# Segment maxima of attention logits: one VectorE instruction per chunk in place of scaled copies by ScalarE and a wide maximum

## The reference, cut to what matters

```python
h = x @ Wn.T + bn
e = edge_attr @ We.T + be
a = jax.nn.leaky_relu(jnp.sum((xj + ee) * attn, axis=-1), 0.01)   # xj = h[src]: one logit per edge
m = jax.ops.segment_max(a, dst, num_segments=N)                    # the maximum of each destination
a = jnp.exp(a - m[dst])
```

## Time and profile before

| | us |
|---|---|
| median of three timed runs | 4665.79 |
| the profiled execution, device time | 4637.7 |
| its span, first to last instruction | 4635.9 |
| logits stage, VectorE's first looped expand to its last reduction | 2416.29 to 2899.99 |
| VectorE busy from 2416 to 2900 | 362.95 |
| ScalarE busy in the same stretch | 356.56 |

### The profile page before, as it was taken

One profiled execution on the slowest core, in us unless ns is written; L12 is line 12 of the kernel. 1 busy time (PEld: TensorE's weight loads), 2 busy tenths in 40 slices (PEclk: granted clock), 3 DMA queues, 4 the chain that ended last, 5 costly groups with the idle time before them and its releaser, 6 DMA issues. The chain is left out here.

```text
span 4635.9 us, 88448 instructions
## 1 busy us (share of the span) xinstructions
PE 3555.2 (77%) x19416; PEld 2665.9 (58%) x19417; DVE 2679.8 (58%) x9145; ACT 1686.4 (36%) x5377; POOL 1075.3 (23%) x828
## 2 busy tenths in 40 slices
PE   5555558888887759999973333689999699998978
PEld 4333337777776658878862222578888344444444
DVE  7999989999987751112237777777766400000523
ACT  1555532334444430000027776577775100000110
POOL 1888888888881000000000000000000000000000
PEclk9999999999998879999985555899999899999989
DMA  3444434567776664435535554443332163442064
GB/s 103 110 114 113 110 75 125 154 196 210 207 215 236 239 220 119 133 110 153 135 116 173 160 156 142 133 139 119 119 102 68 37 221 122 169 155 70 1 253 138
DMA packets 435572, 656.94 MB, mean 142 GB/s; under 512 B 97532, under 2 KB 291767, under 8 KB 435362
## 3 DMA queue, kind: packets, MB, share of 16 engines
q1 hardware_dynamic: 354306, 526.63, 36.9%
q10 hardware_dynamic: 53040, 121.95, 7.2%
q0 software_dynamic: 28144, 7.36, 2.4%
HBM read 438.84 MB, written 216.02 MB: 141 GB/s over the span
## 5 line engine op out<-in xcount | busy, mean ns | idle before, releaser
L989 POOL DMA_INDIRECT slots<-all_B,put_index x800 | 1051.9, 1315 | 342.9 <-issue 238.3
L1725 POOL DMA_DIRECT2D out_dram<-all_B x7 | 8.6, 1222 | 2231.6 <-DVE all_B L1709 2231.6
L965 PE MATMUL put_ps<-put_right_in,put_left_in 128*128 128x125 f32 x2380 | 350.5, 298 | 140.9 <-ACT put_left_in L835 140.3
L765 DVE TENSOR_SCALAR put_hot<-all_iota_bf,put_words_in 128x125 bf16<-128x125 bf16 x2400 | 443.3, 310 | 3.3 <-DMA put_words_in<-slots 3.3
L1220 PE MATMUL lm_ps<-lm_v,lm_node 125*128 x1220 | 169.9, 184 | 328.7 <-DVEq L1087 126.9
L1185 ACT ACTIVATE lm_raised<-lm_hot,srt_words 128x125 f32<-128x125 bf16 x1200 | 360.3, 385 | 140.5 <-DVE lm_top L1100 64.6
L965 PEld LDWEIGHTS put_ps<-put_right_in,put_left_in 128*128 128x128 f32 x2380 | 306.6, 204 | 169.7 <-ACT put_left_in L835 159.7
L835 ACT CAST put_left_in<-put_hot 128x640 f32 (+1 forms) x238 | 172.6, 725 | 633.2 <-issue 316.2
L2262 DVE TENSOR_TENSOR upd_pre<-upd_po,upd_bias 125x512 f32<-125x512 f32 x25 | 17.3, 692 | 630.2 <-PE upd_po L2193 630.2
L1835 PE MATMUL att_ps<-att_right,att_left 128*125 128x125 f32 x2380 | 313.1, 285 | 67.0 <-ACT att_right L1856 63.6
L969 PE MATMUL put_ps<-put_right_out,put_left_out 128*128 128x125 f32 x2380 | 345.9, 298 | 0.7 <-DVE put_right_out L773 0.6
(11 more groups left out here) (346 smaller groups left out, 5967.7 us busy)
## 6 DMA issues: line engine op xcount, KB each, us to landing
c_T<-counts SPq DMA_DIRECT2D x255, 312.5 KB, 2.9
pair<-put_T ACTq DMA_DIRECT2D x125, 625.0 KB
hot<-put_hot SPq DMA_DIRECT2D x480, 160.0 KB
att_ring<-hot SPq DMA_DIRECT2D x240, 320.0 KB, 3.2
all_A<-in_edge_attr_dram SPq DMA_DIRECT2D x100, 448.0 KB
lm_planes<-src_rows SPq DMA_DIRECT2D x123, 320.0 KB, 3.7
counts<-put_T ACTq DMA_DIRECT2D x125, 312.5 KB
lm_hot<-hot SPq DMA_DIRECT2D x120, 320.0 KB, 3.0
```

Source lines behind the costliest of these rows:

```text
L765: ins = v.tensor_scalar(hot[:, h, t, c * S:c * S + P], k["iota_bf"][:, :], words_in[:, j, c, t:t + 1], None, ALU.is_equal)
L965: ins = t_.matmul(tile(1, c), left_in[:, c, :], right_in[:, c, :], start=False, stop=False, skip_group_check=True)
L989: nc.gpsimd.indirect_dma_start(slots, bass.IndirectOffsetOnAxis(index[:, C * g + j:C * g + j + 1], 0), stage[:, C * g + j, :], None).then_ ...
```

## The change

VectorE reads the bf16 one-hots itself. `greater(g)` now issues ten instructions: `tensor_scalar` (times logit) in a block's first group, else `scalar_tensor_tensor` (times logit, then maximum with `lm_top`, in place). ScalarE's loop, the tile `raised` and the semaphore `lifted` are gone. SP's turn has another order: it announces the planes of group g+1 right behind the load of planes g+3, then waits for `grouped` (VectorE's own maxima of group g-3), and loads the hot rows of group g+1, where it had loaded those of g+2.

```diff
@@ sync
-                for j in range(2):
-                    load_hot(j, j)
+                load_hot(0, 0)
...
                         load_planes(g + 3, j + 3)
-                        sp.wait_ge(lifted, g + 1)
-                        sp.sem_inc(passed, 1)
-                        if not last or j < 2:
-                            load_hot(g + 2, j + 2)
                         sp.wait_ge(landed[(j + 1) % RING], 16 * (i + (j + 1) // RING) + 16)
                         sp.sem_inc(arrived, 1)
+                        sp.wait_ge(grouped, g)
+                        sp.sem_inc(passed, 1)
+                        if not last or j < 3:
+                            load_hot(g + 1, j + 1)
                         sp.wait_ge(hot_landed[j], 16 * i + 16)
                         sp.sem_inc(hot_arrived, 1)
@@ vector
                 def greater(g, first):
-                    lift = raised[:, ds(g % 2, 1), :].rearrange("p a n -> p (a n)")
-                    dve.wait_ge(lifted, g + 3)
+                    dve.wait_ge(hot_arrived, g + 1)
                     dve.wait_ge(grouped, g + 2)
-                    if first:
-                        ins = v.tensor_copy(top8[:, :], lift)
-                    else:
-                        ins = v.tensor_tensor(top8[:, :], top8[:, :], lift, ALU.max)
+                    for c in range(G):
+                        one = hot[:, ds(g % RING, 1), c * S:c * S + P].rearrange("p a n -> p (a n)")
+                        at, best = logit[:, ds(G * g + c, 1)], top8[:, c * P:(c + 1) * P]
+                        if first:
+                            ins = v.tensor_scalar(best, one, at, None, ALU.mult)
+                        else:
+                            ins = v.scalar_tensor_tensor(best, one, at, best, ALU.mult, ALU.max)
                     ins.then_inc(grouped, 1)
@@ scalar
-                act.sem_inc(lifted, 2)
-                with act.Fori(0, turns_of(act, k)) as i:
-                    for j in range(RING):
-                        g = RING * i + j
-                        act.wait_ge(ready, g + 1)
-                        act.wait_ge(hot_arrived, g + 1)
-                        act.wait_ge(grouped, g + 1)
-                        for c in range(G):
-                            ins = nc.scalar.activation(raised[:, j % 2, c * P:(c + 1) * P], hot[:, j, c * S:c * S + P], ACT.Copy,
-                                                       scale=logit[:, ds(G * g + c, 1)])
-                        ins.then_inc(lifted, 1)
```

More of the change, by code:

```diff
@@ L1003, in phase_logits @@
         node = s.sb("node", [L, 2, G * L], bf16)
-        raised, top8, tops = s.sb("raised", [L, 2, G * P]), s.sb("top8", [L, G * P]), negated
+        top8, tops = s.sb("top8", [L, G * P]), negated
         v3, rest, z = s.sb("v3", [P, NB, 3], bf16), s.sb("rest", [P, NB]), s.sb("z", [L, G])
@@ L1018, in phase_logits @@
         split, chain_sem = s.sem("split"), s.sem("chain")
-        expanded, looked, summed, ready, lifted, grouped = (
-            s.sem(n) for n in ("expanded", "looked", "summed", "ready", "lifted", "grouped"))
+        expanded, looked, summed, ready, grouped = (
+            s.sem(n) for n in ("expanded", "looked", "summed", "ready", "grouped"))
         joined, passed, turned, ended = (s.sem(n) for n in ("joined", "passed", "turned", "ended"))
```

## The result

| | before | after |
|---|---|---|
| timed median, us | 4669.93 | 4853.98 |
| profiled execution, device time, us | 4637.7 | 4856.24 |
| logits stage, first looped expand to last reduction, us | 484 | 657 |
| VectorE busy in the stage, us | 363 | 528 |
| ScalarE busy in the stage, us | 357 | 0 |

The ratio of the times is 1.0395, with a 95% interval of 1.0362 to 1.0428: slower by 4.0%, 184 us. The kernel before was timed once more beside the new one, hence 4669.93 in place of 4665.79. Its run of 5393.38 us was a slow one, which the median holds and the ratio leaves out.

A forecast was written before the change was run, and what follows sets the result against it. Before, VectorE and ScalarE pace the logits stage in a ring through SyncE; after, VectorE alone. Groups 461.5 + first groups 119.5 + block ends 67.2 - 0.3 = 648 us against 484: +164, 4830 us, range 4785 to 4875.

The forecast's parts named there:

- Ten chunks: VectorE's ten narrow instructions per group: starts 0.26 us apart, 2.68 us in all, bounds 1.72 and 3.44.
- The start and the turn: VectorE's step: 0.45 us from last logit instruction's start to first chunk, 0.45 us idle behind the last chunk.
- The first group's: A block's first group, multiply only: 4.78 us, with 2.55 for ten chunks; times 25 is 119.5 us.
- rival 3: bf16 input makes chunks start 0.17 us apart, ten take about 1.9 us: -95 us, 4735; chance 2%.
- Block ends: VectorE's reduction at a block's end stays: 2.47 us, 0.15 ahead, 0.63 behind; 2.80 more, 24 times, 67.2 us.
- The sum: Logits stage built from VectorE's steps: 648 us against 484, +164 us, 4830 on the timed median.
- SyncE's new order: SyncE's changed turn costs nothing: hot rows issued about 15 us ahead, landing in 3.0; planes covered.
- a ring with ScalarE: Logits stage before: VectorE waits 57.5 us for SyncE, SyncE 299 for ScalarE, ScalarE 112 for VectorE.
- Hidden sequencer work (1): VectorE's address work stays hidden: group 4.18 us, stage 573 us, +89, 4755; chance 4%.
- Chunks that don't overlap (2): Each VectorE chunk waits for the one ahead to end, costing 0.344 us: +91 us more, 4921; chance 4%.
- late hot rows (4): Hot-row loads, issued one group nearer their use, exposed 3.0 us in each of 119 groups: +357, 5187; chance 1%.

The follow-up runs named there:

- e3: The changed kernel with all chunks reading one constant tile and fixed logit columns, no register instruction ahead of a chunk: 4724.45 us, one execution.
- E5: The kernel before, with SyncE announcing the planes of group g+1 before it waits for ScalarE's copies: 4580.80 us, ratio 0.9877.
- e4: The changed kernel with SyncE's old sequence, planes of group g+1 announced last in its turn: 4911.32 us, ratio 1.0500.
- e1: The changed kernel with two wide VectorE instructions (multiply, then maximum) in place of ten narrow ones: 4780.73 us, ratio 1.0238.

## Why the prediction held, point by point

**The account of the 174 us.** The change is two edits of opposite sign. SyncE's new sequence by itself takes 484 to 422 us, -62. The ten fused chunks take that to 657, +235. Of these, 551 - 422 = 129 stay when no addresses are computed (the datapath's part: 2.68 us for ten against 1.46 for one wide maximum, 2.03 against 0.81 in a first group), and 106 are the sequencer's register instructions and loop turn. The split holds for these variants; e3 also took the reading of the ring away.

**Ten chunks** were put at 2.68 us from a neighbouring loop. They took 2.76. The starts were the expected 0.26 apart but for one, between the fifth and the sixth chunk, which was 0.34 (in the step at 2593.68 us); ten chunks take 2.76 or 2.77 in 83 steps. In e3 that gap is gone and ten take 2.68, so it comes with the computed addresses or the ring; which of the two is open. The mixed types changed nothing, as argued from the earlier trace rows.

**The start and the turn** were put at 0.45 and 0.45. The start measured 0.46. The turn was 0.51 behind fused chunks and 0.31 behind a first group's, 42.4 / 93 = 0.46 on average, so that the mean came out close is in part luck. There was luck in the source as well: the profile puts the idle time of line 1898 down to a wait for line 1909, and I read it as sequencer work. Here it is "issue", and e3 shows that it is the sequencer's; what it was at line 1898 no run tested.

**The first group's** 4.78 us measured 2591.89 - 2587.22 = 4.67, as the turn behind it had 0.31 us idle and not 0.45. Its 2.55 us for ten chunks came out exactly. The working there names 0.15 us as line 765's distance and rival 3 names 0.17; with that line's median duration of 253 ns it is (1.72 - 0.253)/9 = 0.16. The sum uses neither. **Block ends** came out as before: 2.46 and 0.62 us.

**The sum** had the stage at 648 us, measured 657; +164, measured +174 in the stage and +184 in the timed medians (4853.98 against the 4830 forecast). Of the 24 us short, 4 are the base (4669.93 against 4665.79) and 10 the stage, of which the chunks' 0.08 us make 94 x 0.08 = 7.5. The last 10 are not located: the profiled executions can't place them, since they differ by 34.5 us ahead of the stage alone.

**SyncE's new order, "at nothing"**, was right for the change: no wait for hot rows, and 0.3 us for planes. But I had read VectorE's 57.5 us of wait on SyncE as part of a ring with ScalarE, ending only with ScalarE's work. E5 shows that the place of one announcement in SyncE's turn made it. The planes had landed by then: with the announcement first, SyncE's queue shows 0.7 us of wait for planes in the whole stage. The sum was not touched, because I built the stage anew from VectorE's steps instead of subtracting waits; what I missed is that the part I priced at nothing is worth 62 us in the kernel before, and that without it (e4) the change would have lost 5% and not 4%.

**Rivals.** Hidden sequencer work (1) falls by the 0.46 us of start and 0.51 of turn that show in a step. Chunks that don't overlap (2) fall by the 0.26 us between starts. With them falls the first half of the rule of the Trainium skill (VectorE: DVE Perf Modes, "The DRAIN you can't avoid"), while its second half, that an operation which is not held starts earlier, is what this trace has. A faster chunk through bf16 (3) falls by 344 ns, and late hot rows (4) by the absence of any wait.

## What to carry to other kernels

Before fusing wide work into one narrow instruction per chunk, multiply the distance between starts of such instructions in this very kernel by their number, and add the address work ahead of the first and behind the last: at 125 elements, ten chunks took 3.73 us of a step, of which about 1 us was address work, and two wide passes took 3.33, of which 0.46 stood ahead of them (e1). When a queue waits for several things in turn, an announcement that is already due should stand ahead of a wait for something else. The size of a DMA queue's wait does not tell: SyncE stood 299 us before, still 235 in e5, and 471 in the changed kernel. Look at what stands behind the wait, and whether an engine waits for it. Build a stage's time from the steps of the engine that will set it, and check what becomes of each wait on its own.

## What the runs showed of the hardware

- A VectorE instruction with two inputs and a pointer scalar on 128x125 lasts 344 ns and starts 0.26 us behind the one ahead of it, whether its first input is float32 or bf16, and whether its addresses are fixed or computed (with computed ones, one of the nine distances was 0.34). The one-input form with float32 output takes 286 ns, 277 in e3; ten take 2.55 us with two register instructions ahead of each, 2.03 without.
- How much of the loop's turn is seen depends on what runs ahead of it: none behind an instruction of 1.46 us, 0.51 us behind ten of 0.34 us with computed addresses, 0.40 behind five, 0.31 behind ten of 0.29 us, and none behind ten of 0.34 us whose own addresses are fixed.
- TensorE's granted clock stood at 0.50 (1.2 GHz) through this stage in all eight kernels, with the same 166 us of TensorE work in stages of 421 to 717 us. In an unchanged earlier phase its mean was 0.91 and 0.89 in two executions, which went with 37 us.
